# Looks ahead and layers between the gram steps in the last group, and another first transfer, in a one-core recommendation tower

## The reference

```python
e = jnp.stack([tbl_k[ids[:, k]] for k in range(26)], axis=1)          # (2048, 26, 128)
combined = jnp.concatenate([dense[:, None, :], e], axis=1)            # (2048, 27, 128)
interactions = jnp.einsum('bnd,bmd->bnm', combined, combined)
z = jnp.concatenate([dense, interactions[:, triu_i, triu_j]], axis=1) # pairs n < m
h = jnp.concatenate([z, dense], axis=1)                               # 607 columns
h = jnp.maximum(h @ W_top1 + b_top1, 0.0)                             # 512
h = jnp.maximum(h @ W_top2 + b_top2, 0.0)                             # 256
y = h @ W_top3                                                        # 1
```

## Time and profile before

| | |
|---|---|
| median of 3 runs | 385.69 us (384.72 to 385.83) |
| the profiled execution | 386.84 us, of which the span of the trace is 384.9 us |
| busy: PE, PE weight loads | 343.2 us (89%), 304.9 us (79%) |
| busy: POOL, DVE, ACT | 251.9 us (65%), 193.3 us (50%), 125.5 us (33%) |
| DMA | 49.57 MB, mean 129 GB/s |

### The profile page before, as it was taken

The page is one execution under the profiler, slowest core; times in us unless marked ns, Lnnn a source line. Parts: engine busy times, 40 slices in busy tenths (PEclk is TensorE's granted clock), DMA queues, the critical chain, the costliest instruction groups (busy, mean ns, idle before and its releaser), DMA issues.

```text
span 384.9 us, 13108 instructions
## 1 busy us (share of the span) xinstructions
PE 343.2 (89%) x6048; PEld 304.9 (79%) x6048; DVE 193.3 (50%) x94; ACT 125.5 (33%) x211; POOL 251.9 (65%) x267
## 2 busy tenths in 40 slices
PE   0787877889999999999999999999999999965995
PEld 0787767788888988889888988989888988854763
DVE  2799997577424872269243962288334942000000
ACT  2344432343233423343223423343223423322122
POOL 5777887777777777777777777777777777100200
PEclk9999999999999999999999999999999999968999
DMA  8996698253624362264525362256325332321300
GB/s 166 251 219 179 171 296 252 58 192 94 188 57 161 108 203 56 56 200 120 154 58 192 82 198 58 80 181 163 101 56 192 85 86 58 135 55 53 126 11 0
DMA packets 30869, 49.57 MB, mean 129 GB/s; under 512 B 17500, under 2 KB 17636, under 8 KB 30687
## 3 DMA queue, kind: packets, MB, share of 16 engines
q1 hardware_dynamic: 22494, 31.82, 27.7%
q0 software_dynamic: 8320, 16.92, 17.0%
HBM read 38.21 MB, written 10.49 MB: 127 GB/s over the span
## 4 chain that ended last, share of the span: by engine, by line
PE 69%; POOL 17%; issue 8%; DVE 3%; DMA 1%; ACT 1%; DVEq 0%
PE look_ps L309 26%; POOL rows L290 17%; PE mid_ps L339 12%; PE layer_ps L356 11%; PE layer_ps L365 7%; PE mid_ps L321 7%; PE layer_ps L353 4%; DVE match L450 3%; PE layer_ps L372 2%; DMA rows<-in_table,index 1%; DMA index<-in_index 1%; ACT hidden L515 0%; ACT hidden L521 0%; ACT turned L495 0%; ACT y_row L528 0%
## 5 line engine op out<-in xcount | busy, mean ns | idle before, releaser
L290 POOL DMA_INDIRECT rows<-in_table,index x256 | 248.7, 971 | 79.3 <-issue 77.7
L450 DVE TENSOR_TENSOR match<-look_ids,row_number_ps 125x2048 fp32r<-125x2048 int32 x80 | 181.8, 2287 | 126.0 <-PE look_ps L309 119.4
L309 PE MATMUL look_ps<-match,table_high 125*128 125x256 f32 x640 | 164.1, 294 | 21.3 <-DVE table_low L458 19.1
L309 PE MATMUL look_ps<-match,table_low 125*128 125x256 f32 x640 | 157.8, 284 | 0.3 <-issue 0.3
L309 PEld LDWEIGHTS look_ps<-match,table_high 125*128 125x128 f32 x640 | 123.3, 193 | 26.8 <-issue 16.8
L309 PEld LDWEIGHTS look_ps<-match,table_low 125*128 125x128 f32 x640 | 123.6, 193 | 0.0
L339 PEld LDWEIGHTS mid_ps<-turned 128*32 128x32 f32 x4096 | 45.6, 110 | 26.6 <-issue 22.7
L339 PE MATMUL mid_ps<-turned 128*32 128x27 f32 x4096 | 54.8, 196 | 12.5 <-issue 7.4
L488 ACT COPY turned<-look_ps 128x512 f32<-128x512 f32 x40 | 31.8, 799 | 68.3 <-PE look_ps L309 68.3
L495 ACT COPY turned<-mid_ps 128x512 f32<-128x512 f32 x64 | 42.9, 671 | 21.9 <-PE mid_ps L321 17.7
L356 PE MATMUL layer_ps<-pairs,w_pairs_sb 117*128 117x256 f32 x192 | 48.0, 386 | 0.0
(11 more groups left out here) (21 smaller groups left out, 44.8 us busy)
## 6 DMA issues: line engine op xcount, KB each, us to landing
look_ids<-in_look_rows SPq DMA_DIRECT2D x40, 256.0 KB
scratch<-grams SPq DMA_DIRECT2D x8, 864.0 KB
rows<-in_table,index POOLq DMA_INDIRECT x256
scratch<-grams SPq DMA_DIRECT2D x8, 416.0 KB
pairs<-scratch SPq DMA_DIRECT2D x92, 29.2 KB
grams<-in_table SPq DMA_DIRECT2D x4, 448.0 KB
pairs<-in_table SPq DMA_DIRECT2D x3, 448.0 KB
hidden<-in_table SPq DMA_DIRECT2D x3, 448.0 KB
```

The lines of the kernel that those rows point to most:

```text
L290: pool.indirect_dma_start(out=rows[j % 2][:, at, :], out_offset=None, in_=tables[GATHERED[at]], in_offset=bass.IndirectOffsetOnAxis(ap=ind ...
L309: last = nc.tensor.matmul(look_ps[pair % 2][:, r % 2, :], part[0:table_rows, r, c, :], match[number % 2][0:table_rows, c, :], start=(c == ...
L450: nc.vector.tensor_tensor(match[number % 2][0:table_rows], look_ids[b][0:table_rows, r % 2].unsqueeze(1).broadcast_to(shape), row_number_p ...
```

## The change

Three edits. In the last round (g = 7) all remaining turns 1 to 3 and looks 7 to 9 follow the gram steps of group 6 at once, and the layers of group 5 move behind them, in pieces, between the gram steps of group 7. The numbers of the `mid_ps` rotation and ACT's copies follow that order, and the store of group 5's output moves behind the last repack in SP's list. At the start the first raw table is issued before the first look's ids, and `index` third.

```diff
             if k >= STEPS and g + 1 == groups:
-                return first + (9, 11, 12, 13)[k - STEPS]
+                return first + (10, 11, 12, 13)[k - STEPS]
...
             if g + 1 == groups:
-                return first - PERIOD + (8, 10, 14, 15)[k]
+                return first - PERIOD + (8, 9, 14, 15)[k]
...
+            load_raw(0)
+            load_look_ids(0, 0)
             sp.dma_start(index[:].rearrange("p a b -> p (a b)"), index_t).then_inc(index_in, 16)
-            load_look_ids(0, 0)
-            load_raw(0)
             load_look_ids(1, 0)
             load_raw(1)
...
-                if g >= 2:
+                if g >= 2 and g + 1 < groups:
                     store_y(g - 2)
...
             repack(groups - 1)
+            store_y(groups - 3)
             store_y(groups - 2)
             store_y(groups - 1)
...
-            for g in range(1, groups):
+            for g in range(1, groups - 1):
...
-            gram(groups - 1, 0)
-            turn(groups - 1, 4)
-            gram(groups - 1, 1)
-            turn(groups - 1, 5)
-            turn(groups - 1, 6)
-            turn(groups - 1, 7)
-            gram(groups - 1, 2)
-            gram(groups - 1, 3)
+            g = groups - 1
+            for k in range(STEPS):
+                gram(g - 1, k)
+                turn(g, k)
+                look(g, AHEAD + k)
+            layer1(g - 2, 0)
+            layer1(g - 2, 1)
+            gram(g, 0)
+            layer1(g - 2, 2)
+            gram(g, 1)
+            turn(g, 4)
+            turn(g, 5)
+            turn(g, 6)
+            turn(g, 7)
+            layer1(g - 2, 3)
+            gram(g, 2)
+            layer2(g - 2)
+            gram(g, 3)
+            layer3(g - 2)
...
+            take_gram(g - 1, 3)
+            take_turned(g, 3)
+            take_look(g, 4)
+            relu1(g - 2, 0)
+            take_gram(g, 0)
+            take_gram(g, 1)
+            take_turned(g, 4)
+            take_turned(g, 5)
+            take_turned(g, 6)
+            take_turned(g, 7)
+            relu1(g - 2, 1)
+            take_gram(g, 2)
+            relu2(g - 2)
+            take_gram(g, 3)
+            copy_y(g - 2)
```

More of the change, by code:

```diff
@@ L414, in _ @@
                     layer3(g - 2)
[L415 to L425, removed]
-            gram(groups - 1, 0)
-            turn(groups - 1, 4)
-            gram(groups - 1, 1)
-            turn(groups - 1, 5)
-            turn(groups - 1, 6)
-            turn(groups - 1, 7)
-            gram(groups - 1, 2)
-            gram(groups - 1, 3)
+                turn(g, 4)
+                look(g + 1, 0)
+                look(g + 1, 1)
+                turn(g, 5)
+                look(g + 1, 2)
+                turn(g, 6)
+                look(g + 1, 3)
+                turn(g, 7)
+                look(g + 1, 4)
+                look(g + 1, 5)
+            g = groups - 1
[8 more added lines that the diff above has]
+            gram(g, 1)
+            turn(g, 4)
+            turn(g, 5)
+            turn(g, 6)
+            turn(g, 7)
+            layer1(g - 2, 3)
[3 more added lines that the diff above has]
+            layer3(g - 2)
             for g in (groups - 2, groups - 1):
@@ L562, in _ @@
                     relu2(g - 2)
-                if g + 1 == groups:
-                    put_dense(g)
                 take_gram(g - 1, 3)
@@ L569, in _ @@
                     copy_y(g - 2)
[L570 to L586, removed]
+                take_turned(g, 4)
+                take_look(g + 1, 0)
+                take_turned(g, 5)
+                put_dense(g)
+                take_turned(g, 6)
+                take_look(g + 1, 1)
+                take_turned(g, 7)
+                take_look(g + 1, 2)
+            g = groups - 1
+            take_gram(g - 1, 0)
+            take_turned(g, 0)
+            take_gram(g - 1, 1)
+            take_turned(g, 1)
+            take_look(g, 3)
+            take_gram(g - 1, 2)
+            take_turned(g, 2)
+            put_dense(g)
+            take_gram(g - 1, 3)
[4 more added lines that the diff above has]
+            take_gram(g, 1)
+            take_turned(g, 4)
+            take_turned(g, 5)
+            take_turned(g, 6)
+            take_turned(g, 7)
+            relu1(g - 2, 1)
[3 more added lines that the diff above has]
+            copy_y(g - 2)
             for g in (groups - 2, groups - 1):
```

## The result

The change runs in 382.82 us (median of 8 runs, 381.89 to 384.17); the kernel before, run between them on the same chip, in 386.54 (median of 8, 384.72 to 390.06). The ratio is 0.9895, interval 0.9856 to 0.9934: about 1% faster, and the interval leaves out "no change". The forecast was 383.1, a gain of 2.6 on the 385.69 known then; the gain measured is 3.7 in medians, and since the median of the kernel before rose to 386.54 with more runs, part of the closeness of 383.1 to 382.82 is luck. The two profiled executions, 383.74 after and 386.84 before, differ by 3.1, as do their spans (381.8 and 384.9). The two terms of the sum need looking at one by one, since a right sum can hide two wrong terms.

The account below looks back on a forecast made before the run. Bound by POOL's gathers behind `index` to about 91 us, then PE, short of instructions at the end. Profiled 386.84 + 4.8 (start) - 7.4 (end) = 384.2; median 385.69 - 2.6 = 383.1, range 379.6 to 387.8.

Parts of the forecast that it names:

- What bounds the kernel: POOL's gathers behind `index` up to about 91 us, then PE, with 10.5 us lost at the end, mostly awaiting instructions.
- The end, 7.4 to 7.7 gained: Group 5's layers behind the looks: 11.8 regained less 3.05 and 1.0 gives 7.7, between 4.5 and 8.5; 7.4 taken.
- the 11.8 that could be regained: End of the kernel: 10.5 us lost from gram(7, 0) to gram(7, 3), plus 1.3 of layer1 at the lower clock.
- the bare steps: gram(6, 1 to 3), left without layers ahead of them: 0.1 to 1.4 us lost for each, 1.0 taken in all.
- the 1.3 for layer1 at the lower clock: Behind the gaps of group 7, layer1's first six products took 2.77 instead of 1.46 us; this would be regained.
- the 3.05 "lost again": Group 7: 0.85 missing between gram(7, 0) and gram(7, 1), 2.2 behind gram(7, 1), at 3.8 us for 256 instructions.
- 2.2 are missing: Turns behind gram(7, 1): it and some 0.4 of the turns make 1.6 us of the 3.8 for 256 instructions.
- Return of the products: From gram(7, 3) to layer1 of group 7: PE's cover is 15.0 against at most 15.3, so a wait of at most 0.3.
- The start, +4.8: `index` behind 756 KB lands at 7.7, not 2.88; first gather, 64th and PE at 91 move by 4.8 (3.6 to 6.0).
- The first (the start costs nothing): Opening: small `index` overtakes the bigger loads or later gathers catch up, so only the end counts: 378.3; 1 in 10.
- The second (the clock falls in group 1, from a wait of 5 us at 80): Group 1: PE waits some 5 us for gathers, then looks run at the lower clock, 4.3 more: 387.4; 2 in 10.
- The third (the gaps stay with the gram steps): End: gaps aren't fetches or spacing doesn't relieve them; only 2.0 regained, the start costs 4.8: 388.5; 1 in 10.

Follow-up runs that it names:

- e2: The kernel before with only the change's new order of SP's first transfers (raw table, first look's ids, `index`): 391.27 us, ratio 1.0106 to the kernel before.
- e6: The change with `index` issued second, behind the first raw table but ahead of the first look's ids: 381.44 us, ratio 0.9832 to the kernel before.
- e4: The kernel before with its last gram step of group 7 done six times into the same place, 1280 more PE instructions: 407.0 us in one run.
- e1: The change with SP's first transfers in the old order (`index`, first look's ids, raw table): 378.92 us, ratio 0.9779 to the kernel before.
- e8: e1 without the 16 gathers of the last 128 samples, whose turns use an earlier tile's rows: 377.82 us, ratio 0.9779 to the kernel before.
- e7: e1 run once more, unchanged, beside e5: 379.72 us, ratio 0.9788 to the kernel before.
- e3: The change with `index` first, then the raw table, then the first look's ids: 379.17 us, ratio 0.9782 to the kernel before.
- e5: e1 with one layer1 piece of group 5 earlier and two turns between gram(7, 0) and gram(7, 1): 381.77 us, ratio 0.9851 to the kernel before.

## Why the prediction was right

*What bounds the kernel.* Right. That `index` is on the chain up to 91 us is shown by e2 and e6, where its landing alone moved the time. That the end's gaps are instructions which come too late is shown by e4 for their period and by e1 for their cure; but the largest of them, 2.78, points to a packet that passed only behind the writes to `scratch`, which the prediction did not see.

*The end, 7.4 to 7.7 gained.* Right in its mechanism but for that first gap, the total too low: 8.4 up to gram(7, 3) and 0.9 behind it make 9.3, which is about the 11.8 that could be regained less some 2.3 in group 7 and 0.5 in the bare steps, and 0.4 more, since the 1.3 for layer1 at the lower clock had left out its first two products. Where the 3.05 "lost again" were placed was wrong twice. "2.2 are missing" in the turns behind gram(7, 1) measured 0.24, and gram(7, 2), which should have been covered, had 1.30; the rest is within gram(7, 0) and gram(7, 1), which took 1.49 and 1.68 instead of 1.29, and the two rows of gram(7, 2), 1.50 together. The failed step is that I let a block of 256 begin with each gram step and gave each 3.8 of its own. A block may be shorter when longer ones stand ahead of it: in e8 the one that ends 6 transposes behind gram(7, 1) took 2.0 us (333.29 to 335.33, by the count of instructions) without a gap, behind blocks of 6.9 and 3.1. And the borders lie elsewhere: the turns' gap comes after 6 of 16 transposes, and the next after 108 of gram(7, 2)'s matmuls, 20 + 16 + 216 = 252 instructions on. Single blocks can also be later than 3.8: the one that ends at 346.31 lasted 5.4 (346.31 - 340.91), with its gap of 1.30, where e1 has 0.18 and e7 none at the same matmul. Which traffic makes one late by so much was not tested. The bare steps, "I take 1.0", cost 0.5: 5.46 for the three (1.83, 1.81, 1.82) for 4.96 before (1.91, 1.76, 1.29). Only the last of them had been short, so there was less to lose than the prediction thought.

*Return of the products.* Right: 15.0 expected from gram(7, 3) to layer1 of 7, 14.5 measured, with no DMA in the brackets of the last row shown above.

*The start, +4.8.* Right in its mechanism, mis-sized: the landing was taken in the middle of its bounds, 7.7, and it came at the low one. The first gather started at 6.83, +3.66, half a microsecond behind the match that the load ahead of `index` releases. PE's shift at the end of group 1 was POOL's, 3.56. But by gram(6, 0) it had become 6.15, with about 1.5 from the clock and 1.1 from groups 3 to 5. In medians the start costs 4.1 by e2 (386.54 x 0.0106) and 4.5 by the change against e1 (386.54 x (0.9895 - 0.9779)). So the 4.8 was nearly met by terms other than those that I gave for it, and in the profiled pair a start too dear by 1.4 hid an end too good by 1.9 (9.3 for 7.4): that the sum came out is luck to that extent.

*The rivals.* The first (the start costs nothing) has fallen with e2 and e6. The second (the clock falls in group 1, from a wait of 5 us at 80) came in part, in another place and at about a third of the size: no wait at 80, one of 2.44 at 94.66, and 1.5 us lost at the lower clock, where I had 4.3 in all. Since e7 has that without the new start, it is not the start's alone. The third (the gaps stay with the gram steps) has fallen with e1 and e4. That the raw table's earlier landing counts nothing is shown by e3.

*What stays open.* The 1.1 us that groups 3 to 5 take longer after the change (no more than two executions of the same work differ by), half of e5's loss, whether moving the writes to `scratch` alone would cure the gap of 2.78, what decides whether the clock falls behind a wait of 2.2 to 2.5 us, and why one block came 1.4 later than the rate of e4.

The best version is the end of the change with the opening of before (e1, 378.9; e7, 379.7): 2.2% faster than the kernel before, and 1% faster than the change as made.

## What to carry to other kernels

Where small matmuls stand in a row, count PE's instructions, weight loads too: here 256 of them took 3.7 to 4.0 us where block followed on block with the DMA queues nearly idle, so mix them with long products until blocks that follow on one another hold that much work, look for large transfers that run beside them, and lay out the blocks by the instruction count, not from where a step begins. An edit that does two things wants two runs: here one half gained 2.2% and the other took 1.1% of it back. In an opening, put what the longest chain waits for first, however small it is.

## What was not expected of the hardware

PE's idle "issue" gaps in gram steps need no traffic beside them: with the DMA queues nearly idle a block of 256 instructions still took 3.73 to 4.01 us. With the DMA engines 0.94 busy beside it, an instruction packet came only after the traffic, twice, and the gap was 2.8. One program's clock fell to 1.2 GHz behind a wait of 2.30 us in one execution, while it stayed at 2.4 GHz behind 2.39 us in another.
